# The diagonals of weight scales of a decoder layer: computed on GpSimd, or kept in device memory and loaded

## The reference

```
x  = LN(x  + rms_norm(lightning_attention(rot(x Wq), rot(x Wk), x Wv)) Wo)
x  = LN(x  + expert(x))                  # int8-like smooth quantised gated linear layers
x  = LN(x  + y / rms(y)),  y = (silu(x Wg^T) * (x Wu^T)) Wd^T
```

```
vals = LUT[nibbles of packed]             # 16 values: 0, 0.5, 1, ... 6 and their negatives
W[o, i] = vals[o, i] * scale[i // 128, o]
```

## Time and profile before

| | |
|---|---|
| median of 3 runs | 800.64 us (799.73 to 802.24) |
| profiled execution | 798.36 us, its span 796.6 us |
| TensorE busy | 725.3 us, 91% |
| VectorE, ScalarE, GpSimd busy | 472.4, 358.0, 200.7 us |
| moved by DMA | 41.18 MB, 52 GB/s in the mean |

### The profile page before, as it was taken

One profiled execution on the slowest core, in us unless ns is written; L12 is line 12 of the kernel. 1 busy time (PEld: TensorE's weight loads), 2 busy tenths in 40 slices (PEclk: granted clock), 3 DMA queues, 4 the chain that ended last, 5 costly groups with the idle time before them and its releaser, 6 DMA issues.

```text
span 796.6 us, 11725 instructions
## 1 busy us (share of the span) xinstructions
PE 725.3 (91%) x4662; PEld 584.0 (73%) x4662; DVE 472.4 (59%) x918; ACT 358.0 (45%) x572; POOL 200.7 (25%) x235
## 2 busy tenths in 40 slices
PE   4899998999999898579899999999999999999993
PEld 3688777877787786357777777777777777788883
DVE  4568668764677767766736458655568464632314
ACT  5345453357353733563524472545353635531214
POOL 0454344354453559711201000211000111000000
PEclk9999999999999998669999999999999999999998
DMA  9500101002300320130001130030130030100201
GB/s 329 186 16 3 51 2 41 15 1 71 116 14 1 102 72 2 53 106 1 2 26 53 53 106 0 1 133 1 53 106 1 10 122 1 53 0 1 106 0 54
DMA packets 25408, 41.18 MB, mean 52 GB/s; under 512 B 5002, under 2 KB 7690, under 8 KB 25226
## 3 DMA queue, kind: packets, MB, share of 16 engines
q1 hardware_dynamic: 23194, 37.40, 13.9%
q10 hardware_dynamic: 2160, 3.02, 1.1%
HBM read 28.88 MB, written 11.53 MB: 51 GB/s over the span
## 4 chain that ended last, share of the span: by engine, by line
PE 61%; DVE 23%; ACT 9%; DMA 2%; issue 2%; POOL 1%; ACTq 0%; DVEq 0%; POOLq 0%
PE ps L1645 22%; PE ps L1659 12%; PE ps L1281 10%; PE ps L1365 3%; DVE small L413 3%; PE ps L1320 2%; PE ps L525 2%; PE ps L534 2%; DMA rms_col<-in_L_attn_rms_w_dram 2%; DVE masked L1200 2%; DVE act_s L406 1%; PE ps L1348 1%; DVE w L406 1%; DVE weights L738 1%; ACT w L276 1%
## 5 line engine op out<-in xcount | busy, mean ns | idle before, releaser
L1645 PE MATMUL ps<-x2T_hi,weights 128*128 128x512 f32 x704 | 217.4, 390 | 0.0
L1645 PEld LDWEIGHTS ps<-x2T_hi,weights 128*128 128x128 f32 x704 | 132.3, 188 | 26.8
L1645 PE MATMUL ps<-x2T_lo,weights 128*128 128x512 f32 x352 | 141.6, 402 | 0.9 <-DVE x2T_lo L1544 0.9
L1659 PE MATMUL ps<-weights,h_hi 128*128 128x512 f32 x352 | 110.8, 396 | 1.8 <-DVE h_lo L1538 1.8
L1554 DVE TENSOR_TENSOR silu<-ps,silu 128x512 f32<-128x512 f32 x44 | 30.3, 689 | 134.1 <-PE ps L1645 127.1
L1281 PE MATMUL ps<-wqkv_lo,xT_hi 128*128 128x512 f32 x192 | 80.9, 421 | 9.8 <-DVE wqkv_lo L1149 5.8
L1468 ACT ACTIVATE silu<-ps 128x512 f32<-128x512 f32 x44 | 26.2, 596 | 114.9 <-PE ps L1645 114.9
L1645 PEld LDWEIGHTS ps<-x2T_lo,weights 128*128 128x128 f32 x352 | 66.2, 188 | 14.7 <-DVE x2T_lo L1544 1.2
L1659 PEld LDWEIGHTS ps<-weights,h_hi 128*128 128x128 f32 x352 | 64.8, 188 | 15.5 <-DVE h_lo L1538 2.5
L1281 PE MATMUL ps<-wqkv_hi,xT_lo 128*128 128x512 f32 x192 | 76.0, 396 | 0.0
L1281 PE MATMUL ps<-wqkv_hi,xT_hi 128*128 128x512 f32 x192 | 75.9, 395 | 0.0
(11 more groups left out here) (181 smaller groups left out, 1381.0 us busy)
## 6 DMA issues: line engine op xcount, KB each, us to landing
w<-in_fside_BxS2xS_dram SPq DMA_DIRECT2D x4, 1024.0 KB, 5.2
x_dram<-xb SPq DMA_DIRECT2D x4, 1024.0 KB, 4.3
xc<-x_dram SPq DMA_DIRECT2D x4, 1024.0 KB, 5.5
x_in<-in_x_dram SPq DMA_DIRECT2D x15, 256.0 KB, 3.4
xb<-x_dram SPq DMA_DIRECT2D x3, 1024.0 KB, 5.5
out_dram<-xc SPq DMA_DIRECT2D x3, 1024.0 KB, 4.8
z<-in_x_dram SPq DMA_DIRECT2D x3, 768.0 KB, 4.9
x_dram<-z SPq DMA_DIRECT2D x3, 768.0 KB, 3.5
```

The source lines that it names most:

```text
L1645: last = nc.tensor.matmul(dst[:, :], lhs, rhs, start=(k == 0 and n == 0), stop=(k == NK - 1 and n == 2))
L1659: last = nc.tensor.matmul(ps[c][:, :], lhs, rhs, start=(it == 0 and n == 0), stop=(it == NI - 1 and n == 2))
```

## The change

GpSimd computes no diagonal any more. Two arrays in device memory hold them all: diag_gu (four groups of 128 rows by 2816 halves, a row of 128 x 2816 elements plus 128 spare) and diag_dn (eleven of 128 by 512).

- At start GpSimd sets values_dn to zero. SP stores these zeros over both arrays in seven transfers (zero_diagonals), behind the load of the expert's weights and ahead of the chunk loop. ScalarE waits for these stores before it first writes values_dn.
- The scales are copied from the inputs onto the diagonals, device memory to device memory, element by element (store_diagonals): one transfer for each of the 15 groups, 2816 elements for a gate/up group and 512 for a down group, issued by SP in chunks 1 to 10.
- Each piece's diagonal is loaded into its slot by SP (load_diagonal), with a semaphore for each slot. In SP's turn of chunk 14 it waits for the copies and for x chunk 15's transposes, loads 0 to 3, waits for chunk 14's attention and loads 4 to 9. 10 to 30 follow the load of the second expert's weights, each waiting for the piece ten (or so) earlier; the x2 store stands between 22 and 23. The last four are loaded beside the FFN.
- The loads of the scales, the 16-bit identity, scale_columns and scale_cols are gone.

```
+ZERO_STORES = NK + 3
+X2_STORE_PIECE = 22
+DIAGONALS_AT = {n: (n - 1,) for n in range(1, 5)} | {n: (2 * n - 6, 2 * n - 5) for n in range(5, 10)} | {10: (14,)}
...
+    def zero_diagonals(self, sp):
+        zeros = self.values_dn[:, :].bitcast(F16)
+        sp.wait_ge(self.zeros_set, 1)
+        for g in range(NK):
+            sp.dma_start(self.diag_gu[g, 0:P * GU_W].rearrange("(p n) -> p n", n=GU_W), zeros).then_inc(self.zeros_stored, 16)
+        for first in range(0, NI, 5):
+            its = min(5, NI - first)
+            sp.dma_start(self.diag_dn[first:first + its, 0:P * E].rearrange("i (p n) -> p i n", n=E),
+                         zeros[:, 0:its * E].rearrange("p (i n) -> p i n", n=E)).then_inc(self.zeros_stored, 16)
...
+    def store_diagonals(self, sp, scales, g):
+        sp.wait_ge(self.zeros_stored, ZERO_STORES * 16)
+        if g < NK:
+            dst = self.diag_gu[g, 0:P * (GU_W + 1)].rearrange("(p q) -> p q", q=GU_W + 1)[:, 0:GU_W]
+            dst = dst.rearrange("p (t n) -> p t n", n=P)[:, :, 0]
+            src = scales[0][g].rearrange("(t p) -> p t", p=P)
...
+        sp.dma_start(dst, src, allow_slow_non_contiguous=True).then_inc(self.diagonals_stored, 16)
...
+    def load_diagonal(self, sp, m):
         kind, where, k, tiles, _ = PIECES[m]
         before = [n for n in range(m) if DIAG_OF[n] == DIAG_OF[m]]
         if before:
-            self.wait_product(pool, before[-1])
+            self.wait_product(sp, before[-1])
...
-        self.nc.gpsimd.tensor_tensor(diag, ident, cols.unsqueeze(len(shape) - 1).broadcast_to(shape), ALU.mult)\
-            .then_inc(self.diag_done, 1)
+        sp.dma_start(dst, src).then_inc(self.diag_in[DIAG_OF[m]], 16)
...
         sp.dma_start(expert.w[:, :, :], w_rows[0]).then_inc(expert.w_in, 16)
+        weights.zero_diagonals(sp)
         for n in range(CHUNKS):
...
+            for g in DIAGONALS_AT.get(n, ()):
+                weights.store_diagonals(sp, scales, g)
+            if n == CHUNKS - 2:
+                sp.wait_ge(weights.diagonals_stored, (NK + NI) * 16)
+                wait_full(sp, "xT", CHUNKS - 1)
+                for m in range(DIAGS):
+                    weights.load_diagonal(sp, m)
+                wait_full(sp, "attn", CHUNKS - 2)
+                for m in range(DIAGS, DIAGS + MORE_DIAGS):
+                    weights.load_diagonal(sp, m)
...
-        sp.wait_ge(expert.x2_done, NC)
-        sp.dma_start(x2_v[0], xb[:, :, :]).then_inc(x2_stored, 16)
+        for m in range(DIAGS + MORE_DIAGS, FIRST_BESIDE + DIAGS):
+            weights.load_diagonal(sp, m)
+            if m == X2_STORE_PIECE:
+                sp.wait_ge(expert.x2_done, NC)
+                sp.dma_start(x2_v[0], xb[:, :, :]).then_inc(x2_stored, 16)
...
-            if n == CHUNKS - 2:
-                weights.diagonals(pool, 0)
-                weights.diagonals(pool, 1)
             wait_drained(pool, "attn", n)
...
             if n == 0:
                 project(1, 0)
-                scale_columns()
                 project(1, 1)
```

More of the change, by code:

```diff
@@ L97 @@
 HALVES = GU_TILES * GU_HALVES + NK * DN_HALVES
-SCALES = (NK * GU_TILES, NI * NK)
+GU_W = GU_TILES * P
 QMAX = 127.0
@@ L655, in __init__ @@
         self.attention_drained = [sem(f"ps{n}_drained") for n in range(6)]
-        self.diag_done, self.hi_done = sem("w_diag_done"), sem("w_hi_done")
+        self.hi_done = sem("w_hi_done")
+        self.zeros_set, self.zeros_stored, self.diagonals_stored = (sem("w_zeros_set"), sem("w_zeros_stored"),
+                                                                    sem("w_diagonals_stored"))
+        self.diag_in = [sem(f"w_diag{n}_in") for n in range(DIAGS + MORE_DIAGS)]
         self.x1_first_stored, self.x1_stored = sem("x1_first_stored"), sem("x1_stored")
@@ L685, in down @@
         return self.parts(PIECE_OF["down", it, 0])
-    def diagonals(self, pool, m):
+    def zero_diagonals(self, sp):
[13 more added lines that the diff above has]
+            src = scales[0][g].rearrange("(t p) -> p t", p=P)
+        else:
+            dst = self.diag_dn[g - NK, 0:P * (E + 1)].rearrange("(p q) -> p q", q=E + 1)[:, 0:E]
+            dst = dst.rearrange("p (t n) -> p t n", n=P)[:, :, 0]
+            src = scales[1][g - NK].rearrange("(t p) -> p t", p=P)
+        sp.dma_start(dst, src, allow_slow_non_contiguous=True).then_inc(self.diagonals_stored, 16)
+    def load_diagonal(self, sp, m):
         kind, where, k, tiles, _ = PIECES[m]
@@ L691, in diagonals, with wait_diagonal @@
         if before:
-            self.wait_product(pool, before[-1])
+            self.wait_product(sp, before[-1])
         diag = self.diags[DIAG_OF[m]]
         if kind == "gate_up":
[L695 to L699, removed]
-        else:
-            cols = self.scale_cols[:, SCALES[0] + where * NK:SCALES[0] + (where + 1) * NK]
-            shape = [P, NK, P]
-            ident = self.expert.ident.unsqueeze(1).broadcast_to(shape)
-        self.nc.gpsimd.tensor_tensor(diag, ident, cols.unsqueeze(len(shape) - 1).broadcast_to(shape), ALU.mult)\
-            .then_inc(self.diag_done, 1)
+            dst = diag[:, 0:2 * tiles].rearrange("p (h t) n -> p h (t n)", h=2)
+            src = self.diag_gu[k, 0:P * GU_W].rearrange("(p h n) -> p h n", h=2, n=GU_W // 2)
+            src = src[:, :, 2 * where * P:(2 * where + tiles) * P]
+        else:
+            dst = diag.rearrange("p t n -> p (t n)")
+            src = self.diag_dn[where, 0:P * E].rearrange("(p n) -> p n", n=E)
+        sp.dma_start(dst, src).then_inc(self.diag_in[DIAG_OF[m]], 16)
+    def wait_diagonal(self, pe, m):
+        pe.wait_ge(self.diag_in[DIAG_OF[m]], 16 * sum(DIAG_OF[n] == DIAG_OF[m] for n in range(m + 1)))
     def product(self, pe, m):
@@ L978, in scale_values @@
                 if first < last:
+                    if start > 0:
+                        act.wait_ge(weights.zeros_stored, ZERO_STORES * 16)
                     part = slice(first - lo, last - lo)
@@ L1087, in rotate @@
                                         ALU.mult).then_inc(kd_done, 1)
+        nc.gpsimd.memset(weights.values_dn[:, :].bitcast(F32), 0.0).then_inc(weights.zeros_set, 1)
         pool.wait_ge(tab_in, 16)
@@ L1284, in project @@
                 last.then_inc(full[BANK_OF[u]], 1)
[L1286 to L1293, removed]
         def chunk(n):
@@ L1436, in sync_program @@
                 sp.dma_start(xb[:, :, :], x1_v[b]).then_inc(expert.x1_in, 16)
+                if b == 1:
+                    for m in range(FIRST_BESIDE + DIAGS, len(PIECES)):
+                        weights.load_diagonal(sp, m)
             if b < B:
@@ L1527, in pool_program @@
         for b in range(B - 1):
-            beside = place(steps, {}, b, lambda m: weights.diagonals(pool, m + DIAGS) if m + DIAGS < len(PIECES) else None)
+            beside = place(steps, {}, b)
             for at in range(3 * NI):
```

30 lines of the change are left out of this document (7 added, 23 removed).

## The result

The changed kernel takes 806.96 us (median of five runs, 805.62 to 809.08) against 800.64 for the kernel before (five runs, 798.86 to 802.24): ratio 1.0078, 95% interval 1.0052 to 1.0104. The profiled execution took 805.62 us with a span of 803.7, so 7.3 us more than the profiled one of before. As built, the change makes the kernel 0.8% slower.

What follows compares the result with a forecast made beforehand. TensorE's work, plus the few places where it waits or runs at low clock, bounds the kernel. +12.7 for the zero stores less 4.5 for the diagonals gives +8.2: 806.6 profiled, median 808.8, range 803 to 820.

Steps and rivals of the forecast that it cites:

- A: The forecast case: x chunk 2's load waits behind the zero stores, +8.2 us, range 804 to 817, chance 0.68.
- Part 1: Zero stores, 4.33 MB ahead of x chunk 2 on SP's queue: 11.2 us shift plus 1.5 of low clock, +12.7 us.
- or the issue itself is late: Sign to look for: the x load behind the zero stores lands some 20 us after issue, or is issued late.
- Part 2: Start-up scale columns removed: next projection up to 1.8 us sooner, all lost in the wait for x chunk 2, gain nothing.
- Part 3: Element stores in chunks 1 to 10: 12.5 ns an element, 2.2 us a gate/up group, hidden, cost 0.
- rival C: Element stores are dear: decides at 17.2 us a group, 98 ns per element and engine; +20 us, 829; chance 0.13.
- Part 4: GpSimd's 35 diagonals removed: VectorE and GpSimd waits around the piece stage shrink, gain 4.5 us, bounds 1.5 and 7.5.
- If the low clock of that stage ends sooner, up to 3 us more: Possible extra gain of up to 3 us in the stage where GpSimd's diagonals went, from TensorE's clock.
- The rule of the Trainium skill: VectorE instructions with two SBUF inputs and GpSimd ones reading SBUF exclude each other; DMA contends with no engine.
- Part 5: Loads of 35 diagonals of 128 KB by SP: issued early enough to be hidden, cost 0, up to 2 us.
- Rival D: GpSimd's waits are replaced by waits for loads and ScalarE, gain 0.5 us only: 812.8, chance 0.09.
- Rival B: Stores and loads pass each other in the queue, so zeros don't delay x chunk 2: -4.9 us, 795.7, chance 0.10.

Runs made afterwards that it cites:

- e1: Changed kernel with the seven zero stores moved behind the load of x chunk 3, one turn into SP's loop: 797.75 us, ratio 0.9983.
- e2: Changed kernel with only the 1.44 MB of down zeros ahead of the loop, the other 2.88 MB moved into turn 1: 804.93 us.
- e9: Changed kernel plus products nobody reads on TensorE's queue where it waits in chunk 15 and the piece stage: 803.59 us, ratio 1.0054.
- e8: Kernel before, diagonals still on GpSimd, plus only products nobody reads on TensorE's queue in chunk 15 and the piece stage: 799.53 us, ratio 0.9991.
- e5: Changed kernel with zero stores in turn 1 and x chunks 2 and 3 loaded ahead of residuals and expert's weights: 794.01 us, ratio 0.993.
- e7: e5 with each gate/up group's 2816 element transfers issued 12 times over, the further ones to device memory nobody reads: 943.37 us.
- e3: Changed kernel with 31 idle GpSimd products of the diagonals' shape that read SBUF, results unread: 812.21 us.
- e4: Changed kernel with two idle GpSimd memsets, reading nothing, in place of each of the 31 idle products of e3: 808.24 us.
- e6: e5 plus products nobody reads on TensorE's queue where it waits between 308 and 342 us: 787.98 us, ratio 0.987.

## Why the prediction was right, and where not

The case was A, "x chunk 2 behind the zeros": 808.8 predicted, 806.96 measured; in profiled executions +8.2 predicted, +7.3 measured.

**Part 1, the zero stores: +12.7 predicted, +12.2 measured.** Landing at 51.7 predicted, 50.3 measured: the 4.33 MB landed in 10.4 us (39.3 to 49.7) and not in 11.6, at up to 425 GB/s where I had taken 384 and 350, so the transposes are 9.9 us late, below my lower bound of 10.7. The clock cost more than the 1.5 I took: 2.3 us (12.2 at x chunk 3 less 9.9), since ten output products and the transposes ran at the lower level. The two errors nearly cancel. e1 shows that the queue is the cause, e2 that the size is, e9 that nothing of it comes back. Part of the delay passed in SP itself, ahead of the issue, which is the point "or the issue itself is late": 11.63 us for the issue of three stores. The cover of 0.4 us was one execution's too: in e8, whose start-up is that of before, the same load ends a wait of 0.5 us.

**Part 2, start-up: 0 predicted, 0 measured, and 3.1 us once the stall is gone** (e5). My row gave up to 1.8. The mean over the five executions with e5's start-up is 2.2; that e5 also orders its loads otherwise, and that they spread over 2.8 us, leaves open how much scale_columns alone cost.

**Part 3, element stores: 0 predicted and measured, with a price that holds for a group alone.** The 12.5 ns were not a rate but the packets' share of the engines' time. As a rate they came out right by luck: the first two groups of the changed kernel pass in 2.2 and 1.9 us, 12.7 and 10.7 ns per element and engine, against 2.2 us predicted. The third and fourth, with x loads close around them on the queue, take from 97.1 to 105.5, 23.8 ns, and in a full queue it is 25.3 (e7). The estimate by the Trainium skill in the prediction (DMA: Bandwidth & Descriptors, section Specifications), 4.4 us a group, fits the full queue (4.5) and not a group alone; that a read-modify-write is the reason no run here shows. From issue to landing a group of 2816 takes 6.9 us in the median and one of 512 takes 3.8. The threshold of rival C was wrong too. The cover is not 17.2 us of a chunk but what SP has between its wait for the words and the transposes of x chunk 5: in e5 89.8 - 76.35 - 2.3 = 11.1 us, or 63 ns per element instead of 98. Already the kernel before issues that load at 79.4 for a use at 92.9. Still, 4.5 us are under 11.1, so C was out in the kernel as built.

**Part 4, the diagonals: 4.5 predicted; 7.5 in the stage, 5.2 up to the end.** The mechanism is shown by e3 and e4, and 4.8 us is its size there; the 43.1 to 43.9 us of the six other executions, 4.4 to 5.2 less than before, say the same. So the 4.5 were right, and the 3 us beyond them in the profiled execution are its luck with the clock, for which I have no cause. What I mis-sized is what comes next. "If the low clock of that stage ends sooner, up to 3 us more" came true in the profiled execution (chunk 15's output product took 2.8 us and not 5.0), and I did not see that the head of the FFN would then begin at the low clock and give 2.3 us back. In the six others it gives back 2.0 (450.0 us from the x2 transposes to the end, before 448.0), so that 3 us of gain are the usual and 5.2 this execution's. The rule of the Trainium skill (SBUF - State Buffer, section Who interferes with whom) held in both halves: GpSimd's memsets, which read nothing, left VectorE's operations at 0.16 us, and so did the diagonals' loads: the moments at 340.68 took 0.16 us while the DMA engines were busy for 0.75 of the time (340 to 345 us).

**Part 5, the loads: 0 to 2 predicted, 0 measured.** No wait of TensorE ends with a diagonal's DMA. Rival D (0.5 us of gain in all) is out with that. Rival B is what e1 and e5 had to build: 795.7 was its price, and e5, which has no stall, takes 794.0.

## What to carry to other kernels

Before a kernel adds transfers to a queue, ask which load stands behind them and by how much it is early: here it was 0.4 us, and 4.33 MB of zeros for diagonals that nobody loads before chunk 14, some 250 us later, cost 12 us where they stood and nearly nothing one turn of the loop later (x chunk 3 is 0.2 us late in e1). A gain on an engine that isn't the bound shows only as far as the next bound; when that is TensorE's clock, a few products that nobody reads can be worth as much as the change (6 us on top of e5, nothing in the kernel before). And price small transfers by how many pass in a time, alone and in a busy queue, not by the share of engine time that they show. Last, a stage read from one profiled execution can be off by the clock's luck: here 7.5 us against some 5 in six others.

## What the runs showed of the hardware that I had not expected

- Transfers of single two-byte elements within device memory pass at 25.3 ns per element and engine in a full queue, and the engines show 35% busy meanwhile (e7). A group of 2816 alone passes at about half of that, with the engines 86.5% busy. What fills the rest in the full queue is open. SP is held up too: each issue of 2816 more elements in e7 took 4.5 us in the median, where the changed kernel's took 0.57.
- Stores of zeros from SBUF to device memory ran at up to 425 GB/s, above the 376 and 391 of the earlier trace rows.
- TensorE's clock spreads the executions of one kernel. e5 took 790.8 and 791.0 us at a mean clock of 0.978, 793.2 at 0.973, and 794.9 to 795.6 at 0.969; e9 802 to 804 at 0.983 and 807 to 809 at 0.974 to 0.976. In e5's profiled execution one such place is chunk 6, after a wait of 1.0 us:
```profile
120.00:124.00 4.00, 3.19 (x9) 2.30 (x9) 3.70 (x6) 0.00 (x0) 2.69 (x5) 0.50 0.00 0
```
where e6, with the same program up to there and the same wait, has the full clock:
```profile
120.00:124.00 4.00, 2.86 (x19) 2.55 (x20) 4.00 (x8) 0.00 (x0) 2.76 (x4) 1.00 0.00 0
```
  It costs 2.3 us (23.2 against 20.9 from x chunk 6 to 7). Why it falls in one execution and not in another I can't say, and filler at this place wasn't tried.
